# Layer 0's thinking steps: both products of the four-row block cut in quarters on strips of 32 rows

## What is computed

```python
x_norm = layer_norm(x, in_gamma, in_beta)
thought = x_norm[:, -1, :] @ agg_w + agg_b                 # 4 x 256
for _ in range(K_STEPS):                                   # 4 steps
    t = layer_norm(thought, pn_gamma, pn_beta)
    t = jax.nn.gelu(t @ d1_w + d1_b, approximate=False)    # 4 x 1024
    thought = thought + (t @ d2_w + d2_b)                  # 4 x 256
broadcast = (thought @ bc_w + bc_b)[:, None, :]
gate = jax.nn.sigmoid(x @ gate_w + gate_b)                 # 2048 x 256
out = x + gate * broadcast
# beside it, for the recurrence:
x_proj = (x @ C_w.T + C_b) * jax.nn.sigmoid(x @ D_w.T + D_b)
g = g * A_diag + xt                                        # scan over the tokens
```

## Time and profile before

| | |
|---|---|
| median of 3 runs | 2118.67 us (2117.53 to 2118.79) |
| profiled execution | 2134.49 us, its span 2132.7 us |
| PE busy over the span | 1835.4 us (86%) |
| DVE busy | 1396.8 us (65%) |
| mean granted TensorE clock | 0.918 |
| the four steps | from 39.53 us (first turn) to 112.05 us (turn of the result) |
| `layer0_join` starts on PE | 115.62 us |

### The profile page before, as it was taken

How to read it: one execution, slowest core, us unless ns; L and a number is a source line. 1 busy time by engine, 2 the same in 40 slices (tenths; PEclk the granted TensorE clock), 3 DMA queues, 4 the chain that set the end, 5 groups by cost and what they waited for, 6 DMA issues and landing times. The chain is left out here.

```text
span 2132.7 us, 36972 instructions
## 1 busy us (share of the span) xinstructions
PE 1835.4 (86%) x13816; PEld 1446.0 (68%) x13816; DVE 1396.8 (65%) x2980; ACT 736.7 (35%) x1729; POOL 569.7 (27%) x550
## 2 busy tenths in 40 slices
PE   5953479990899999999999996989997997989995
PEld 2341257770799989998999995455566885767773
DVE  4477255556787777778787876566656778544444
ACT  2222334440333433333334333135534323322231
POOL 1234615551021222212121211632323102511111
PEclk9975569995899999999999998999997996999998
DMA  8419324436000000000000100000001007111114
GB/s 312 145 48 295 117 81 152 136 112 221 1 2 24 2 24 1 24 24 1 24 1 24 33 1 1 1 1 2 2 1 53 28 1 247 60 38 50 51 46 140
DMA packets 102876, 134.74 MB, mean 63 GB/s; under 512 B 11568, under 2 KB 78796, under 8 KB 102192
## 3 DMA queue, kind: packets, MB, share of 16 engines
q1 hardware_dynamic: 91616, 101.89, 15.2%
q0 software_dynamic: 11088, 30.49, 4.0%
HBM read 81.80 MB, written 50.54 MB: 62 GB/s over the span
## 5 line engine op out<-in xcount | busy, mean ns | idle before, releaser
L1119 POOL TENSOR_TENSOR a_rstd<-a_msq,consts 128x8 f32<-128x8 f32 x32 | 52.4, 1637 | 554.1 <-DVE a_msq L1474 554.1
L110 PE MATMUL a_ring<-a_w_hi,l_xnT_hi 128*128 128x256 f32 x512 | 152.0, 297 | 0.0
L110 PE MATMUL a_ring<-a_w_hi,l_xnT_lo 128*128 128x256 f32 x512 | 144.5, 282 | 0.0
L110 PE MATMUL a_ring<-a_w_lo,l_xnT_hi 128*128 128x256 f32 x512 | 144.3, 282 | 0.0
L2468 POOL DMA_INDIRECT l_slots_in<-xn,f_row_of x96 | 98.0, 1021 | 95.1 <-DVE f_row_of L2796 37.0
L3029 POOL DMA_INDIRECT l_pairs_out<-f_yb,f_to_row x96 | 95.6, 996 | 101.1 <-ACT f_yb L3004 69.5
L1431 DVE RECIPROCAL a_rT<-a_rT 128x256 f32<-128x256 f32 x64 | 111.5, 1743 | 0.0
L1720 PE MATMUL b_ring<-b_keys,b_qm 32*128 32x128 f32 (+2 forms) x896 | 91.5, 340 | 14.9 <-DVE b_nm L1933 9.4
L1886 ACT ACTIVATE b_work<-b_ring 128x1024 f32<-128x1024 f32 (+1 forms) x96 | 81.0, 881 | 62.3 <-PE b_ring L1727 61.3
L2923 PE MATMUL f_pgu<-f_gate_up_w,f_xT 128*128 x384 | 95.4, 392 | 6.2 <-ACT f_xT L2984 5.5
L110 PEld LDWEIGHTS a_ring<-a_w_hi,l_xnT_hi 128*128 128x128 f32 x512 | 97.5, 190 | 0.2 <-issue 0.2
(11 more groups left out here) (507 smaller groups left out, 5404.7 us busy)
## 6 DMA issues: line engine op xcount, KB each, us to landing
l_slots_in<-l_zeros SPq DMA_DIRECT2D x4, 3120.0 KB, 22.3
f_xb<-l_slots_in SPq DMA_DIRECT2D x11, 1040.0 KB
f_gate_up_w<-l_pairs_out SPq DMA_DIRECT2D x16, 512.0 KB, 8.8
l_slots_in<-l_zeros SPq DMA_DIRECT2D x3, 1690.0 KB, 18.6
f_xb<-l_slots_in SPq DMA_DIRECT2D x39, 130.0 KB, 2.0
f_down_w<-L_ffn_w_down_dram SPq DMA_DIRECT2D x1, 4096.0 KB
f_gate_w<-L_ffn_w_dram SPq DMA_DIRECT2D x2, 2048.0 KB, 10.5
f_up_w<-L_ffn_w_dram SPq DMA_DIRECT2D x2, 2048.0 KB, 19.7
```

Source lines behind the costliest of these rows:

```text
L110: ins = pe.matmul(out, a, b, start=start and k == 0, stop=stop and k == 2, **kw)
L1119: pool.tensor_tensor(rstd[:], msq[:], core.consts[:, C_HALF:C_HALF + 8], ALU.pow).then_inc(s["rstd_ready"], 1)
```

## The change

Both products of a step are cut into four quarters that write side by side into strips of 32 rows of one PSUM bank.

- Up: for each of the two chunks of channels and each strip j a product 32 rows x 256 columns (the four rows of `tT`, padded with zero columns to 32), so that strip j holds hidden columns 256j to 256j+255. The bias `b1` is laid out in the same way (four loads in place of one), and DVE adds it in one instruction of 128x256 in place of two of 4x512.
- The turn of `hidden`: two of 128x128 in place of eight of 4x128, and Gelu on 128x256 in place of 128x32.
- Down: strip j takes the two chunks of its own quarter, eight products of 256 columns in all; each strip then holds a partial result. ACT copies these (128x256) to SBUF, and one further product with `pick` (ones at rows r, 32+r, 64+r, 96+r of column r) adds them up into `out_rows`.
- No item stands between the down product and the sum; the two items come behind the sum. The bias is added to `thought` ahead of the wait for the rows, not behind it.
- `tT` is set to zero once, and `pick` is made by three small additions.

```diff
+        quarter = self.HIDDEN // 4
+        for j in range(4):
+            sp.dma_start(self.b1[32 * j:32 * j + 32, :],
+                         on_all_partitions(dram["L0_ffn_d1_b"][j * quarter:(j + 1) * quarter], 32)
+                         ).then_inc(self.small_in, 16)
...
-    FIRST, IN_STEP = 5, (1, 1, 1, 2)
+    FIRST, IN_STEP = 5, (1, 1, 1, 0, 2)
...
-                for half in range(2):
-                    for c in range(DC):
-                        ins = pe.matmul(pH[0:B, half, :], tT[:, c, :], w.up[:, c, half * T:(half + 1) * T],
-                                        start=(c == 0), stop=(c == DC - 1))
-                    ins.then_inc(s["h_ready"], 1)
+                for c in range(DC):
+                    for j in range(4):
+                        ins = pe.matmul(p_up[strip(j), :], tT[:, c, :], w.up[:, c, 2 * j * P:2 * (j + 1) * P],
+                                        start=(c == 0), stop=(c == DC - 1), skip_group_check=True)
+                ins.then_inc(s["h_ready"], 1)
...
-                for half in range(2):
-                    pe.wait_ge(s["h_biased"], 2 * b + half + 1)
-                    for h in range(HC // 2):
-                        at = B * (half * (HC // 2) + h)
-                        ins = pe.transpose(hidden_turned[:, at:at + B], hidden[:, half, h * P:(h + 1) * P],
-                                           core.ident[0:B, 0:B])
+                pe.wait_ge(s["h_biased"], b + 1)
+                for n in range(2):
+                    ins = pe.transpose(hidden_turned[:, n * P:(n + 1) * P], hidden[:, n * P:(n + 1) * P], core.ident)
...
-                add_rows(w.down, hT, HC)
+                for k in range(2):
+                    for j in range(4):
+                        ins = pe.matmul(p_down[strip(j), :], hT[:, k, strip(j)], w.down[:, 2 * j + k, :],
+                                        start=(k == 0), stop=(k == 1), skip_group_check=True)
+                ins.then_inc(s["down_ready"], 1)
                 for n in items(done, IN_STEP[3]):
                     project(n)
                 done += IN_STEP[3]
+                pe.wait_ge(s["partial_copied"], b + 1)
+                pe.matmul(out_rows, pick[:], partial[:], start=True, stop=True).then_inc(s["rows_done"], 1)
+                for n in items(done, IN_STEP[4]):
+                    project(n)
...
-                act.activation(hT[:], hidden_turned.rearrange("p (h b) -> p h b", b=B), ACT.Gelu).then_inc(s["h_act"], 1)
+                act.activation(hT[:], hidden_turned.rearrange("p (k n) -> p k n", k=2), ACT.Gelu).then_inc(s["h_act"], 1)
+                act.wait_ge(s["down_ready"], b + 1)
+                act.activation(partial[:], p_down, ACT.Copy).then_inc(s["partial_copied"], 1)
...
+            setup_do(dve.memset(tT[:], 0.0))
...
+            choose(dve.tensor_tensor(pick[:], core.ident[:, 0:B], core.ident[:, 32:32 + B], ALU.add))
...
-                for half in range(2):
-                    dve.wait_ge(s["h_ready"], 2 * b + half + 1)
-                    dve.tensor_tensor(hidden[:, half, :], pH[0:B, half, :], w.b1[:, half * T:(half + 1) * T], ALU.add
-                                      ).then_inc(s["h_biased"], 1)
+                dve.wait_ge(s["h_ready"], b + 1)
+                dve.tensor_tensor(hidden[:], p_up, w.b1[:], ALU.add).then_inc(s["h_biased"], 1)
                 running_sum(2 * b + 1)
+                out_b = Steps(dve, s["out_step"], 1 + 2 * b, 2)
+                out_b(dve.tensor_tensor(thought[:], thought[:], rows[:, 5, :], ALU.add))
                 dve.wait_ge(s["rows_done"], b + 2)
-                out_b = Steps(dve, s["out_step"], 1 + 2 * b, 2)
                 out_b(dve.tensor_tensor(thought[:], out_rows, thought[:], ALU.add))
-                out_b(dve.tensor_tensor(thought[:], thought[:], rows[:, 5, :], ALU.add))
```

More of the change, by code:

```diff
@@ L432, in __init__ @@
         self.up, self.down = st.sb("w1", [P, DC, self.HIDDEN]), st.sb("w2", [P, HC, D])
-        self.cols, self.b1, self.rows = st.sb("cols", [P, 5, DC]), st.sb("b1", [B, self.HIDDEN]), st.sb("rows", [B, 6, D])
+        self.cols, self.b1, self.rows = st.sb("cols", [P, 5, DC]), st.sb("b1", [P, self.HIDDEN // 4]), st.sb("rows", [B, 6, D])
         self.ab, self.out_norm = st.sb("ab", [P, 2, DC, 64]), st.sb("out_norm", [P, 2, D])
@@ L436, in __init__ @@
             "proj_w_in", "small_in", "agg_w_in", "mlp_w_in", "out_norm_in"))
-        self.SMALL = 16 * 14
+        self.SMALL = 16 * 17
     def load(self, sp):
@@ L462, in layer0_mix @@
     sem = st.sem
-    HC = w.HIDDEN // P
     KS = 4
@@ L468, in layer0_mix @@
     thought, tnorm = st.sb("thought", [B, D]), st.sb("tnorm", [B, D])
-    tT, hT, hidden = st.sb("tT", [P, DC, B]), st.sb("hT", [P, HC, B]), st.sb("hidden", [B, 2, T])
+    tT, hT, hidden = st.sb("tT", [P, DC, 32]), st.sb("hT", [P, 2, P]), st.sb("hidden", [P, 2 * P])
+    partial, pick = st.sb("partial", [P, D]), st.sb("pick", [P, B])
     raw, mean, var, rstd = st.sb("traw", [B, 6]), st.sb("tmean", [B, 1]), st.sb("tvar", [B, 1]), st.sb("trstd", [B, 1])
@@ L520, in turn_rows, with strip @@
                 ins.then_inc(s["t_turned"], 1)
+            def strip(j):
+                return slice(32 * j, 32 * j + 32)
             def add_rows(weight, lhs, n_c):
                 for c in range(n_c):
-                    ins = pe.matmul(out_rows, lhs[:, c, :], weight[:, c, :], start=(c == 0), stop=(c == n_c - 1))
+                    ins = pe.matmul(out_rows, lhs[:, c, 0:B], weight[:, c, :], start=(c == 0), stop=(c == n_c - 1))
                 ins.then_inc(s["rows_done"], 1)
@@ L567, in _ @@
                 done += IN_STEP[3]
+                pe.wait_ge(s["partial_copied"], b + 1)
+                pe.matmul(out_rows, pick[:], partial[:], start=True, stop=True).then_inc(s["rows_done"], 1)
+                for n in items(done, IN_STEP[4]):
+                    project(n)
+                done += IN_STEP[4]
             assert done >= ITEMS
@@ L606, in _ @@
                 act.wait_ge(s["h_turned"], b + 1)
-                act.activation(hT[:], hidden_turned.rearrange("p (h b) -> p h b", b=B), ACT.Gelu).then_inc(s["h_act"], 1)
-                for n in items(done, IN_STEP[2] + IN_STEP[3]):
+                act.activation(hT[:], hidden_turned.rearrange("p (k n) -> p k n", k=2), ACT.Gelu).then_inc(s["h_act"], 1)
+                act.wait_ge(s["down_ready"], b + 1)
+                act.activation(partial[:], p_down, ACT.Copy).then_inc(s["partial_copied"], 1)
+                for n in items(done, sum(IN_STEP[2:])):
                     gates(n)
-                done += IN_STEP[2] + IN_STEP[3]
+                done += sum(IN_STEP[2:])
         @block.gpsimd
@@ L622, in _ @@
                 pool.wait_ge(w.out_in, 32)
-                pool.wait_ge(s["h_biased"], 2 * n)
+                pool.wait_ge(s["h_biased"], n)
                 k = n - (KS - SHIFTS) - 1
@@ L651, in copy_turned @@
                 dve.wait_ge(s["t_turned"], n + 1)
-                dve.tensor_copy(tT[:], turned.rearrange("p (c b) -> p c b", b=B)).then_inc(s["t_copied"], 1)
+                dve.tensor_copy(tT[:, :, 0:B], turned.rearrange("p (c b) -> p c b", b=B)).then_inc(s["t_copied"], 1)
             def running_sum(m):
@@ L674, in _ @@
                 setup_do(dve.tensor_scalar(decay[:, c, :], decay[:, c, :], decay_col[:, c:c + 1], None, ALU.mult))
+            choose = Steps(dve, s["pick_step"])
+            choose(dve.tensor_tensor(pick[:], core.ident[:, 0:B], core.ident[:, 32:32 + B], ALU.add))
+            choose(dve.tensor_tensor(pick[:], pick[:], core.ident[:, 64:64 + B], ALU.add))
+            choose(dve.tensor_tensor(pick[:], pick[:], core.ident[:, 96:96 + B], ALU.add))
             dve.wait_ge(s["rows_done"], 1)
```

10 lines of the change are left out of this document (5 added, 5 removed).

## The result

| | before | changed |
|---|---|---|
| median | 2118.10 us (2116.28 to 2118.79, 4 runs) | 2099.28 us (2095.39 to 2104.80, 4 runs) |
| profiled execution, its span | 2134.49 us, 2132.7 us | 2104.80 us, 2102.9 us |
| first turn to the turn of the result | 39.53 to 112.05 us | 38.07 to 94.14 us |
| `layer0_join` starts on PE | 115.62 us | 98.02 us |

The ratio is 0.9916, with a 95% interval of 0.9902 to 0.9930: 14.8 to 20.8 us less. I had predicted 2102.1 us (2096 to 2109).

The account below looks back on a forecast made before the run. PE's time plus about 1.04 us a step was taken as the bound, the chain once products shorten. Steps save 16.86 us, less 0.24 outside, so 16.6: 2118.67 to 2102.1 us, own range 2099 to 2105, wider range 2096 to 2109.

Parts of the forecast that it names:

- The price of strips: Up and down products: each quartered product priced at 1.01 us from the routing stage's trace, in place of about 3.5.
- The worry that strips between full-width products cost more: Up and down products: strips might cost 0.1 to 0.4 us above 1.01, twice a step; part of a rival, chance 0.14.
- the smaller gain: Rival on the thinking steps: dearer Gelu and strips leave only 12 to 14 us gained, 2105 to 2107 us; chance 0.14.
- The chain of the second step: Second thinking step, summed from turn to next turn: 14.19 us in place of 18.37, 4.18 saved.
- the third step: Third thinking step: its second item needs nothing of ACT, so down starts at 7.29 us, 0.44 earlier; 4.62 saved.
- The last: Last thinking step: the final turn waits for PE; 11.65 us for 15.53, 3.88 saved.
- The first step: First thinking step: same work as the second, slow start ahead of the up product and unchanged; 4.18 us saved.
- the three additions for `pick`: DVE ahead of its wait for the first rows: about 0.2 us each, making the chain 0.24 us late.
- The loads of the bias: SP's queue: three further loads, some 1 us more of issuing, hidden, so no cost.
- The bias's addition: DVE, each step: 0.45 us, now made while DVE waits for the rows anyway.
- Nothing was given back behind the stage: Answers a rival on the join and layer 1: another clock phase leaves 8 us or less, 2108 to 2114; chance 0.08.
- The profiled execution: Whole kernel under profile: 2134.49 less 16.6, so 2117.9 us, keeping the 15.8 us above the median.

Follow-up runs that it names:

- e2: The changed kernel again, no edit: median 2125.24 us, ratio 0.9932 to the kernel before; steps 16.56, 14.06, 13.46, 11.60 us.
- e10: The changed kernel run a third time, no edit: median 2100.00 us, ratio 0.9925 to the kernel before; steps 15.60, 14.06, 13.45, 11.60 us.
- e1: The kernel before again, no edit: median 2140.91 us, ratio 1.0001; steps 21.10, 18.37, 18.37, 15.54 us.
- e3: Changed kernel with only the up half kept, down product and late bias as before: median 2130.22 us, ratio 0.9953 to the kernel before.
- e11: Kernel before with only the bias added to `thought` ahead of the wait for the rows: 2114.18 us (one run) beside 2118.03.
- e7: Changed kernel, two items moved ahead of the first step, one fewer behind the sum in three steps, one more in the last: 2126.01 us, ratio 0.9948.
- e8: Changed kernel, two items moved ahead of the first step, none before up, DVE's last recurrence piece behind the chain: 2118.16 us, ratio 0.9915.
- e9: Against e8, a second-step sigmoid moved behind Gelu and copy, bias addition moved ahead of DVE's scan: 2094.90 us, ratio 0.9896 to the kernel before.
- e5: Changed kernel with both quartered products' loops swapped, each strip's two products one behind the other: 2122.59 us, ratio 0.9929 to the kernel before.

## Why the prediction was right

**The price of strips** (1.01 us from the earlier trace rows) measured 1.00. It was the estimate with the greatest weight in the sum, and a row with the same number of columns, strips and entries in another stage carried it. The worry that strips between full-width products cost more has no ground here. Of the 2.38 of the Trainium skill, "TensorE: Matmul & The Clock Gate", Part 3: the trace has 3.53 / 1.00 = 3.5 times for four strips, so its figure for three did not bear on this form, and the smaller gain built on it did not come. Nor did the other part of that rival: Gelu on 128x256 took 0.38 us, as the copy from which I had priced it, and not the 0.69 of the sigmoid.

**The chain of the second step**, after its turn at 55.04, predicted and measured:

| | predicted | measured |
|---|---|---|
| up starts | 2.13 | 2.12 |
| turns start | 5.06 | 4.94 |
| Gelu starts | 7.16 | 7.15 |
| down starts | 7.73 | 7.58 |
| sum starts | 9.30 | 9.16 |
| DVE adds the rows | 10.00 | 9.86 |
| next turn | 14.19 | 14.05 |

Every row is within 0.15. Three small terms were mis-sized: a start behind ACT is 0.05 us after Gelu's end (62.57 to 62.62), not 0.19; an item that follows another product or strips directly takes 1.82 us from start to start (58.16 to 59.98), not 1.92; and the two turns take 0.22 (59.98 to 60.20), not 0.31. In the second step only the first of them lies on the chain. In the third step the down product comes 6.98 us after the turn for 7.29, and the step takes 13.45 for 13.75. The last takes 11.60 for 11.65.

**The first step** was the term that I mis-sized in this profile: 3.28 us saved for 4.18. I had put its slow start ahead of the up product. In the changed kernel's profile the up product at 42.06 still ran at half the clock (1.94 us for 1.07), and the item behind it began slowly (2.18 for 1.98). The other profiles show that when the clock rises differs between executions: the same step of the changed kernel took 16.97, 16.56 and 15.60 us (e2, e10), that of the kernel before 20.25 and 21.10 (e1). The means differ by 4.3 us (20.68 less 16.38), close to the 4.18; but with two and three executions that differ by up to 1.4 us among themselves this settles little. In the first pair the four steps together save 16.45 us, where the sum had 16.86.

**Outside the steps**: the three additions for `pick` are 0.16 us each, and PE's wait ahead of the first turn went from 4.40 to 4.66 us, 0.26 for the predicted 0.24. The loads of the bias cost nothing that can be seen. One term I had not priced: from the turn of the result to the join's start the profiles without the sum by `pick` (before, e1, e3, e11) take 3.57 us each, those with it 3.85 to 3.89 (but for e7, at the low clock there), so the join comes 0.3 us later. The rows of PE and DVE up to the barrier are alike in both; what takes the 0.3 us no run tells.

**What I had not priced**: POOL. In the third step of the changed kernel DVE's timeline has:

```profile
75.03 1.49 DVE L679 TENSOR_TENSOR_SCAN l_gsT<-m_decay,m_drive 128x512 f32<-128x512 f32 x1
76.44 1.43 DVE L707 TENSOR_TENSOR m_thought<-m_thought,m_rows 4x256 f32<-4x256 f32 x1
78.35 0.41 DVE L709 TENSOR_TENSOR m_thought<-m_pS,m_thought 4x256 f32<-4x256 f32 x1 [0.48 <-PE m_pS L578]
```

and POOL's, the four instructions together and then the third of them alone:

```profile
72.93 6.06 POOL L643 TENSOR_TENSOR x<-x,m_out_norm 128x512 f32<-128x512 f32 x4 [5.30 <-DVE m_hidden L704]
...
75.39 2.20 POOL L643 TENSOR_TENSOR x<-x,m_out_norm 128x512 f32<-128x512 f32 x1
```

The bias's addition, which I called hidden, took 1.43 us in place of 0.41. It ended at 77.87, 0.48 before the rows were there; half a microsecond more and the step would have been longer, as it was in e8. The cover that I named, DVE's wait for the rows, was there, but I had reckoned with an addition of 0.45 us and without POOL; that 0.48 us of it was left was luck.

**What reached the end.** The join starts 17.60 us earlier in the first pair of profiles (of which 1.46 lie ahead of the first turn, where the change saves nothing, so that much belongs to the executions) and 16.09 in e1 and e2; the medians differ by 18.8 us, and the ratios of e2 and e10 make 14.6 and 15.9. The intervals of all three ratios hold the predicted 16.6. Nothing was given back behind the stage: from the join to the end e1 and e2 differ by 0.11 us, so that rival fell.

**The profiled execution** was the number that I missed: 2104.80 us, where I had said 2117.9. I had carried over the 15.8 us by which the profile of before stood above its median. A product of layer 1's experts shows where they were. PE's timeline in the kernel before:

```profile
293.51 0.80 PE L2956 MATMUL f_pgu<-f_down_b,f_yb 32*128 32x256 f32 x2
```

in the changed kernel:

```profile
263.19 0.80 PE L2975 MATMUL f_pgu<-f_down_b,f_yb 32*128 32x256 f32 x2
```

and in e11:

```profile
276.11 0.80 PE L2956 MATMUL f_pgu<-f_down_b,f_yb 32*128 32x256 f32 x2
```

From the join's start that is 177.9, 165.2 and 162.6 us. e11 has the code of before in all of this stretch, so 15.3 of these us belong to the execution, or its chip, and not to the kernel. ACT's waits in the attention of layer 1 (waited for: us in total, times, longest) in the profile of before name something outside of the program's engines:

```profile
ACT a_e L891 <- remote: 29.2, 6, 9.6
ACT a_sums L897 <- remote: 24.8, 6, 12.5
```

In e11 the stretch has no such wait. All eight profiles of the two chips on which the kernel before takes 2140 and 2136 us have 181.4 to 183.6 us there, both kernels alike; the chip of e9 to e11, on which it takes 2118, has 158.7 to 162.7. So the 20 us between chips lie in this stretch too. What holds the engines there no run tells; it stays open. Only differences within a chip, or within the stage, were used above.

## What to carry to other kernels

A chain of small products that each fill a few of the unit's columns is worth cutting into strips, but price it along the chain: the strips themselves saved 2.5 us each, and what a partial sum needs behind them (a copy, one more product, a wait for each) took back 1.1 us of it for the down product. When the chain gets shorter than the filler work, look at every filler again: one that stands in front of a chain product costs what it adds to the wait that is there anyway (1.5 us of its 1.9 a step here: the up product starts 2.12 us after the turn with it, 0.61 without), one behind the last product costs nothing as long as it ends under the wait there, and taking that one out brought the clock down and cost more than it saved (e7). And when a profiled execution stands far above the median, find the stretch in which it does before carrying the difference over.

## What the runs showed of the hardware

- Strips of 32 rows hardly depend on the order in which they are written: 1.00 us with the four strips in turn, 1.03 with the two products of a strip one behind the other (e5).
- While POOL adds rows to `x` (two operands in SBUF, 1.27 us for an instruction that meets nothing), a DVE addition of two SBUF operands of 4x256 took 1.43, 1.42 and 1.42 us (changed kernel, e8, e11) for 0.39 to 0.41, and a scan 1.29 to 2.00 for 1.22. In all three the addition ended 0.28 us after the POOL instruction that ran beside it (77.59, 71.57 and 87.65), and that instruction, begun under a scan, itself took 2.20, 2.18 and 2.18 us. In e9, where the addition began 0.24 us before POOL, it kept its 0.41. The addition that reads one operand from PSUM kept its 0.41, and the one with `m_pC` from PSUM its 0.75. The Trainium skill, "SBUF — State Buffer", section "Who interferes with whom", says that a DVE instruction with two inputs from SBUF contends with a GpSimd instruction that reads SBUF, and that such contention is an exclusive lock and not a sharing; the trace agrees, the wait of some 1.0 us being under one POOL instruction.
- The granted clock stayed at 1.00 with PE busy for 10.40 of 11.83 us and its idleness in gaps of 0.33 to 0.60 us (e9), and fell to half with 10.63 busy of 14.05 us and a gap of 2.38 us ahead of each turn (e7). Which of the two, the share or the gap, the chip answers to, these runs don't separate.
- The changed kernel's times fall into pairs in both series in which it takes about 2100 us (the first and e10): 2104.80 and 2103.16 beside 2095.39 and 2095.41; 2103.27 and 2103.17 beside 2096.83 and 2095.87. Of the 8.0 us between a profile of each kind 6.5 lie between the join and layer 1's experts (165.2 and 158.7 us). The cause is open.
